# A fused attention and feed-forward kernel: both transposed-score matmuls of a slot ahead of its two score tiles

## The reference, cut to what matters

```python
q = _proj(Wq, bq, layernorm(x)); k = _proj(Wk, bk, ctx); v = _proj(Wv, bv, ctx)
q, k = _rope(q, 8), _rope(k, 8)                       # per head, 16 channels
scores = einsum('bhqd,bhkd->bhqk', q, k) / sqrt(16)   # 512 x 512 for each of 8 heads
out = einsum('bhqk,bhkd->bhqd', softmax(scores), v)
x = x + tanh(g_xattn) * _proj(Wo, bo, out)
...
h = silu(gate) * up                                   # gate, up: 1408 columns each
y = h @ w_down.T
x = x + tanh(g_ffn) * y / rms(y)
```

## Time and profile before

| | before |
|---|---|
| median of 3 runs | 942.87 us |
| lowest and highest run | 941.97 and 942.91 us |
| span of the profiled execution | 939.5 us |
| TensorE matmuls busy | 880.0 us, 94% of the span |
| VectorE busy | 571.1 us, 61% |
| ScalarE busy | 529.1 us, 56% |

### The profile page before, as it was taken

One profiled execution on the slowest core, in us unless ns is written; L12 is line 12 of the kernel. 1 busy time (PEld: TensorE's weight loads), 2 busy tenths in 40 slices (PEclk: granted clock), 3 DMA queues, 4 the chain that ended last, 5 costly groups with the idle time before them and its releaser, 6 DMA issues. The chain is left out here.

```text
span 939.5 us, 13857 instructions
## 1 busy us (share of the span) xinstructions
PE 880.0 (94%) x4134; PEld 486.0 (52%) x4134; DVE 571.1 (61%) x1024; ACT 529.1 (56%) x991; POOL 220.2 (23%) x196
## 2 busy tenths in 40 slices
PE   4689999999999999999997569999999999999997
PEld 1344544455444445444542356666666666666664
DVE  5878988888888888889994773222322322232112
ACT  3227888788887888887787454224322432252223
POOL 8202343334443343432222750000000000000000
PEclk9559999999999999999999779999999999999999
DMA  6463344444444544344300101000200020001001
GB/s 186 145 183 108 120 121 148 150 126 143 139 127 141 154 127 147 113 130 131 103 25 23 56 1 45 0 1 1 90 1 1 0 89 0 0 2 43 1 1 45
DMA packets 44927, 74.36 MB, mean 79 GB/s; under 512 B 11610, under 2 KB 13914, under 8 KB 44890
## 3 DMA queue, kind: packets, MB, share of 16 engines
q1 hardware_dynamic: 44890, 73.90, 25.6%
HBM read 48.17 MB, written 25.17 MB: 78 GB/s over the span
## 5 line engine op out<-in xcount | busy, mean ns | idle before, releaser
L636 DVE TENSOR_REDUCE row_max<-s_ps 128x1 f32<-128x512 f32 x512 | 330.8, 684 | 61.0 <-PE s_ps L356 57.5
L528 ACT ACTIVATE probs<-st_ps 128x512 f32<-128x512 f32 x512 | 272.8, 599 | 104.6 <-PE st_ps L409 104.1
L356 PE MATMUL s_ps<-k_stack,q_stack 126*128 126x512 f32 x512 | 222.1, 471 | 10.0 <-DMA k_stack<-qk_scratch 9.6
L356 PEld LDWEIGHTS s_ps<-k_stack,q_stack 126*128 126x128 f32 x512 | 100.8, 197 | 148.5 <-DVE row_max L636 87.2
L409 PE MATMUL st_ps<-q_stack,k_stack 128*128 128x512 f32 x512 | 168.0, 408 | 6.2 <-ACT probs L528 3.3
L1113 PE MATMUL gu_ps<-x_head,gu_head 128*128 128x512 f32 x352 | 156.1, 443 | 0.0
L969 DVE TENSOR_TENSOR hidden<-gu_ps,silu 128x512 f32<-128x512 f32 x44 | 30.4, 691 | 202.5 <-ACT silu L1052 202.5
L1052 ACT ACTIVATE silu<-gu_ps 128x512 f32<-128x512 f32 x44 | 26.3, 597 | 204.7 <-PE gu_ps L1116 204.7
L1114 PE MATMUL gu_ps<-x_rest,gu_head 128*128 128x512 f32 x352 | 138.9, 395 | 0.0
L377 PE MATMUL pv_ps<-probs,v_ones 128*32 128x512 f32 x1024 | 136.2, 604 | 0.9 <-ACT probs L528 0.9
L409 PEld LDWEIGHTS st_ps<-q_stack,k_stack 128*128 128x128 f32 x512 | 96.6, 191 | 47.6 <-ACT probs L528 30.2
(11 more groups left out here) (132 smaller groups left out, 935.7 us busy)
## 6 DMA issues: line engine op xcount, KB each, us to landing
qk_scratch<-split SPq DMA_DIRECT2D x32, 512.0 KB, 4.5
k_stack<-qk_scratch SPq DMA_DIRECT2D x192, 64.0 KB, 2.2
q_stack<-qk_scratch SPq DMA_DIRECT2D x64, 128.0 KB, 2.5
xt<-x_dram SPq DMA_DIRECT2D x16, 256.0 KB, 2.9
ct<-ctx_dram SPq DMA_DIRECT2D x16, 256.0 KB, 3.9
cv<-ctx_dram SPq DMA_DIRECT2D x16, 256.0 KB, 2.8
q_stack<-qk_scratch SPq DMA_DIRECT2D x64, 64.0 KB, 2.5
x_res<-x_dram SPq DMA_DIRECT2D x16, 256.0 KB, 5.1
```

The lines of the kernel that those rows point to most:

```text
L356: nc.tensor.matmul(s_ps[n % RING][:], q_stack[p][rows, head, qt * P:(qt + 1) * P], k_stack[p][rows, head // 2, :], start=True, stop=True). ...
L528: nc.scalar.activation(probs[unit % 2][:, slot, k], st_ps[n % RING][:], ACT.Exp).then_inc(expd, 1)
L636: nc.vector.tensor_reduce(row_max[p][:, head, qt:qt + 1], s_ps[n % RING][:], AXIS_X, ALU.max).then_inc(maxed, 1)
```

## The change

In `tensor_step`, the call of `score` that stood ahead of the two transposed-score matmuls is taken out, and the call behind them issues both tiles of the slot. No instruction is added or removed, no tile gets another bank, and the orders on VectorE, ScalarE, GpSimd and SyncE stay as they are.

```diff
                         ahead, tiles = score_tiles(unit, slot)
                         if ahead > left:
                             tiles = []
-                        score(pe, b + ahead, (p + ahead) % 2, tiles[:1])
                         if unit == 0 and slot == 0:
                             pe.wait_ge(max_in[p], (turn_of(b, p) + 1) * 16 * MAX_ROWS)
                         head = (unit // 2) * QUAD + slot
...
                             nc.tensor.matmul(st_ps[n % RING][:], k_stack[p][:, head // 2, kt * P:(kt + 1) * P],
                                              q_stack[p][:, head, :], start=True, stop=True).then_inc(st_done, 1)
-                        score(pe, b + ahead, (p + ahead) % 2, tiles[1:])
+                        score(pe, b + ahead, (p + ahead) % 2, tiles)
                         if unit == UNITS - 1 and slot == 0 and left:
                             turn_max(pe, b + 1, 1 - p)
```

## The result

| | before | after |
|---|---|---|
| median | 942.89 us (4 runs) | 949.94 us (4 runs) |
| lowest and highest | 941.97 and 943.52 | 949.33 and 951.14 |
| span of the profiled execution | 939.5 us | 948.3 us |

The ratio is 1.0072, with a 95% interval of 1.0061 to 1.0084: slower by 7.05 us, where 8.6 were forecast, and inside the range of 946 to 957.

What follows compares the result with a forecast made beforehand. TensorE's own matmul chain was taken as the bound in batches 1 to 12. Loop batches 6.9, batch 13 1.0, batch 14 0.4 and first slot 0.3 sum to 8.6 us, giving 951.5 us, range 946 to 957.

Steps and rivals of the forecast that it cites:

- The order itself: TensorE's matmul order: the same matmuls run with only new neighbours, so the reordering alone costs 0.
- The wait of the last score tile: Double slots without other work: the fourth score tile waits for VectorE's bank, 0.09 us each, four places, 0.36 us a batch.
- Unit 3: Slots 0 to 2 of unit 3: reductions, shuffle and negation move 0.35 us later, 0.18 to spare, so 0.17 us more.
- The loop batch: Each of batches 0 to 12 grows by 0.53 us, 6.9 us in all.
- Batch 13: Batch with weight unpacking on VectorE, which is fed later: 1.0 us more, bounds 0.53 and 1.5.
- Batch 14: Batch with score tiles in three units only, where TensorE waits already: 0.4 us more, bounds 0 and 0.8.
- The first slot: Start of batch 0: a score tile done during the wait for the maxima's DMA now follows it, 0.3 us more.
- The maxima's DMA: DMA of the maxima, issued 0.35 us later, still lands in time with 0.6 us of cover: cost 0.
- the third rival: The maxima's DMA lands over 0.6 us later and each batch pays the excess; for 0.3 us, 955 us; chance 0.02.
- The waits for `k_stack`: Loads of halves of `k_stack` gain room; they held a matmul 0.2 us in all, at best gained: counted 0.
- What would show it: Expected signs: matmul waits listed for score tiles, last score tile 0.32 us behind its neighbour, loop batch 29.3 us.
- The clock: Rival: new waits drop TensorE's clock to 1.2 GHz for one unit a batch, up to 94 us, 1045 us; chance 0.01.

## Why the prediction was right, and where its terms were off

**The order itself, 0: right.** With the shorter reduction the new order costs nothing (28.81 against 28.79 us a batch).

**The wait of the last score tile, 0.09 us in each double slot without other work: right in three of four places.** Units 1 and 2 are longer by 0.11 and 0.09 us (medians of the loop batches: 7.37 to 7.48, 7.04 to 7.13), one such place each. Unit 0 has two, and grew by 0.11 (7.25 to 7.36) instead of 0.18. In its first double slot the second pair of transposed scores already waited for ScalarE before the change: in the earlier trace rows the load came 0.27 us after its engine went idle, and the pair took 0.56 us from 263.69 to 264.25. That wait stands between the first and the last score tile and gave the bank its time: in batch 7 the first double slot grew by 0.01 us, the second one by 0.08. I had read the row for the release and not seen that it was itself a place of the sum.

**Unit 3, 0.17 us: 0.18 measured (7.12 to 7.30), but put together otherwise.** The timelines of TensorE, ScalarE and VectorE after, slots 0 to 2 of unit 3 of batch 7:

```profile
288.94 0.73 PE L408 MATMUL st_ps<-q_stack,k_stack 128*128 128x512 f32 x2
289.52 0.62 PE L356 MATMUL s_ps<-k_stack,q_stack 126*128 126x512 f32 x2
289.98 0.27 PE L362 MATMUL misc_ps<-ident,row_max 128*32 128x128 f32 x1
290.01 0.80 PE L408 MATMUL st_ps<-q_stack,k_stack 128*128 128x512 f32 x2
290.64 0.62 PE L356 MATMUL s_ps<-k_stack,q_stack 126*128 126x512 f32 x2
291.19 1.06 PE L377 MATMUL pv_ps<-probs,v_ones 128*32 128x512 f32 x8
292.19 0.73 PE L408 MATMUL st_ps<-q_stack,k_stack 128*128 128x512 f32 x2
292.76 0.77 PE L356 MATMUL s_ps<-k_stack,q_stack 126*128 126x512 f32 x2
293.37 0.60 PE L385 MATMUL misc_ps<-heads_out,wo 128*128 128x512 f32 x1
...
289.16 0.60 ACT L499 ACTIVATE pv_sb<-pv_ps 128x512 f32<-128x512 f32 x1 [0.79 <-PE pv_ps L377]
289.66 2.06 ACT L527 ACTIVATE probs<-st_ps 128x512 f32<-128x512 f32 x4
...
289.95 1.29 DVE L635 TENSOR_REDUCE row_max<-s_ps 128x1 f32<-128x512 f32 x2 [0.69 <-PE s_ps L356]
...
292.30 1.86 DVE L635 TENSOR_REDUCE row_max<-s_ps 128x1 f32<-128x512 f32 x3
```

The first maximum starts 1.01 us behind the end of the values (1.00 forecast, 0.53 before), and the first one of slot 1, behind shuffle and negation, 3.36 us behind that end, at 292.30, 0.37 later than in the earlier trace rows. The second score tile of slot 2 costs 0.14 us: 292.76 to 293.37 is 0.61 where two matmuls take 0.47. The other part lies one slot earlier. The transposed scores at 290.01 take 0.63 us to the score tile. Two matmuls behind the turn take 0.55: in the earlier trace rows's measure 0.47, and 0.08 that the first of them still waits behind the turn. ScalarE copies `pv_ps` first in slot 0 of unit 3, so its banks come free no earlier, while the transposed scores now come one matmul earlier. The first exponential starts at 289.66 and ends at 290.26; with 0.05 and 0.10 us its bank is written again from 290.41, and the next matmul stands one matmul later, at 290.64. I argued that the exponentials keep their places and left ScalarE's ring out of this slot. The two parts are 0.22 us by these rounded rows, and unit 3 of this batch grew by 0.19 (7.11 to 7.30).

**The loop batch: 0.53 forecast, 0.48 measured.** 13 such batches are 6.9 us by the forecast; batches 3 to 12 grew by 0.41 to 0.54 us each.

**Batch 13: 1.0 forecast, 0.55 measured. Batch 14: 0.4 forecast, with bounds of 0 and 0.8; 0.9 measured.** Its windows differ by 1.24 us (25.68 and 26.92), but they don't hold the same work. They are cut at the first transposed score of a batch, and in the kernel before the first score tile of the batch stands ahead of it. TensorE's timeline before, at that cut:

```profile
462.02 0.50 PE L356 MATMUL s_ps<-k_stack,q_stack 126*128 126x512 f32 x1
```

The window starts at 462.36. In the other batches such a tile falls out at one end and in at the other; batch 15 has no score tiles, so the window of batch 14 held 23 before and holds 24 now. That is 0.34 of the 1.24 us. From the start of batch 13's last values to the start of its own, batch 14 grew from 25.47 us (461.03 to 486.50) to 26.38 (469.11 to 495.49), by 0.91, and by 0.98 against the run that gave it the old order.

The step that failed is the bound of batch 14: "TensorE waits there already" was read as room. TensorE's timeline after, in batch 14 from unit 2 to unit 3:

```profile
488.56 0.40 PE L356 MATMUL s_ps<-k_stack,q_stack 126*128 126x512 f32 x1
489.22 0.50 PE L356 MATMUL s_ps<-k_stack,q_stack 126*128 126x512 f32 x1 [0.26 <-DVE row_max L635]
...
491.82 0.28 PE L362 MATMUL misc_ps<-ident,row_max 128*32 128x128 f32 x1 [0.44 <-DVE row_max L635]
```

The engine that TensorE waits for there is VectorE, which had 25.03 us of work in 25.68, so VectorE's chain counts. The double slot that ends with the values at 489.65 takes 3.61 us instead of 3.09, and the next one, with the turn, 2.86 instead of 2.69: 0.69 of the 0.91 us. VectorE now gets the first score of a double slot 0.47 us later, and in batch 14 no score tile stands between its last maximum and the turn. That this delay is the whole cause is argued from the order and the waits; no run took it away alone. Why batch 13 paid less than forecast was not taken apart.

**The first slot, 0.3: about right.** The first transposed score waits for a DMA in both, and 41 score tiles stand ahead of it before, 40 now. The tile that moved behind the wait is one matmul more in the stage. By the cut it shows as the 0.34 us in the window of batch 14; 0.1 of that is the weight load behind the values, which the window of batch 0 no longer has. Batch 0 was even 0.5 us shorter in the profiled execution (29.57 to 29.06), with a granted clock of 0.92 instead of 0.90; that is not put down to the change.

**The maxima's DMA, 0: right in the loop, wrong in batch 1.** One of the two DMAs issued there took 3.6 us to land, and the first transposed score of batch 2 waited. TensorE's timeline after:

```profile
120.73 0.73 PE L408 MATMUL st_ps<-q_stack,k_stack 128*128 128x512 f32 x2 [0.46 <-DMA q_stack<-neg_max]
```

and the landing of the DMAs of line L248 from 110 to 121 us:

```profile
DMA to landing us min/median/max: 2.2/2.9/3.6
```

This is the third rival, at one batch of sixteen. The forecast took the 2.65 us of a loop batch; at this place one landing took 3.2 us before the change already. Batch 1 went from 28.96 to 29.98 us, 0.46 of it by this wait. It is no accident of one execution: the same place waited 0.33 us in the run with the even slots, 0.32 in the one with the last batches old and 0.20 with 448 keys, and not at all with 384 keys, where the maxima come earlier. A slip in the same paragraph of the prediction changes nothing: the transposed score of that batch stood at 262.75 us, not at 262.5, so it moved a matmul earlier and 0.17 us later, to the 262.6 that the cover was reckoned from.

**The waits for `k_stack`, 0: gained once.** Batch 2 had the one wait of 0.2 us. It is gone, so that batch grew by only 0.19 us.

**What would show it: one sign was wrong.** I expected the waits among TensorE's matmuls to appear in its list of waits. From 128 to 415 us that list is empty after the change. A matmul whose weight load is late is recorded from its natural start, with the wait inside its duration. The signs that worked were the distance between starts and the list of the weight loads.

**The clock** stayed full through every new wait, in the change and in all runs: no row of a loop batch shows less than 1.00. Of the rule of the Trainium skill that the prediction weighed (TensorE: Matmul & The Clock Gate, "A second HAM failure mode: psum-queue depth-cycling"), no run here shows the effect.

In all, 5.0 us in batches 2 to 12 (0.2 in batch 2, 4.8 in the ten others), 1.0 in batch 1, 0.55 in batch 13, 0.9 in batch 14 and 0.34 for the moved first tile, less 0.5 in batch 0, are the 7.3 us of the stage.

The forecast's 8.6 came near that partly by luck. It had the ten loop batches too dear by 0.5 us together, batch 13 by 0.5, batch 2 by 0.3 and batch 0 by 1.0 (0.5 shorter instead of 0.5 longer), and batches 1 and 14 too cheap by 0.5 each. What was right by its working is the loop batch, 0.53 against 0.48 us, which carries two thirds of the cost.

## What to carry to other kernels

Where several engines share rings of few banks, write for each ring the loop of a bank (matmul to reader, the reader, release, next matmul) beside the number of matmuls between two users of it; each order of the producer gives one distance per ring, and it is the shortest distance that waits, not the average load of the reader. VectorE and ScalarE had 14 and 18% of rest in every batch here, and both could be made to hold TensorE up by a regrouping that changed no instruction. When two orders are compared by stage, check that the windows hold the same instructions: here the cut alone moved 0.34 us into one batch. Spread each ring's users evenly, then look at what the moved instruction releases (here the DMAs behind the last transposed score) and at the slots in which a reader has other work first.

## What the runs showed of the hardware

- A bank's loop beyond its reader is 0.43 + 0.05 + 0.10 = 0.58 us at full clock, from the matmul's streaming to the reader, from the reader's end to the weight load, from the load to the next streaming. The last two were read from ScalarE's ring; for VectorE the end of the reduction to the load was 0.06 us (302.15 to 302.21). The sum forecast waits of 0.09 us for VectorE and 0.24 for ScalarE, and 0.09 and 0.25 were measured.
- The profile can count waiting as matmul time: TensorE's busy time in a loop batch rose from 28.78 to 29.28 us with the same instructions, and its list of waits was empty from 128 to 415 us. It isn't always so: in batch 14 waits of 0.26 and 0.44 us are listed.
- The reduction can be cut by a fifth (0.69 to 0.56 us) without any effect on the time where TensorE sets the pace (28.79 us a batch with and without), and by the same cut 7 us disappear where the ring does.
